# A graph-attention kernel with its front ordered anew, its transposes held two units ahead for longer, and its end summed in quarters

## The reference, cut to what matters

```
x = layernorm(x + L0(x, adj))        # masked softmax whose mask, with adj's ones on the diagonal, leaves only the own row
x = layernorm(x + L1(x, adj))

L1: h = x @ W.T + b_W
    e[i, j] = leaky_relu(h[i] @ a1 + h[j] @ a2 + b_a)      # slope 0.2
    p = softmax(where(adj > 0, e, -9e15), axis=1)          # 4096 x 4096
    return p @ h                                           # 4096 x 128
```

## Time and profile before

| | us |
|---|---|
| median of 3 runs | 253.71 (253.17 to 254.16) |
| the profiled execution | 255.0 |
| its span, first to last instruction | 253.2 |
| PE busy | 236.2 |
| DVE busy | 185.3 |
| ACT busy | 154.4 |
| POOL busy | 61.4 |

### The profile page before, as it was taken

How to read it: one execution, slowest core, us unless ns; L and a number is a source line. 1 busy time by engine, 2 the same in 40 slices (tenths; PEclk the granted TensorE clock), 3 DMA queues, 4 the chain that set the end, 5 groups by cost and what they waited for, 6 DMA issues and landing times.

```text
span 253.2 us, 4017 instructions
## 1 busy us (share of the span) xinstructions
PE 236.2 (93%) x1523; PEld 133.3 (53%) x1523; DVE 185.3 (73%) x284; ACT 154.4 (61%) x182; POOL 61.4 (24%) x104
## 2 busy tenths in 40 slices
PE   5959999499999999999999999999999999999980
PEld 4947675245555555555555555555555555555450
DVE  1378787967777777779768776977777778797433
ACT  2468978989067999170489994610899982220032
POOL 3284688999200000003030000002300000032122
PEclk9999999679999999999999999999999999999998
DMA  6999999999999999999589999998499920010102
GB/s 187 365 386 389 383 387 383 387 387 386 385 388 383 380 384 387 387 386 385 64 237 305 332 403 392 387 387 298 114 299 339 397 99 3 1 41 3 41 3 88
DMA packets 40939, 71.76 MB, mean 283 GB/s; under 512 B 5843, under 2 KB 6100, under 8 KB 40916
## 3 DMA queue, kind: packets, MB, share of 16 engines
q1 hardware_dynamic: 40480, 71.33, 79.2%
q10 hardware_dynamic: 436, 0.13, 0.2%
HBM read 69.36 MB, written 2.10 MB: 282 GB/s over the span
## 4 chain that ended last, share of the span: by engine, by line
PE 86%; POOL 3%; ACT 3%; DMA 2%; DVE 2%; issue 2%; ACTq 1%; POOLq 0%; DVEq 0%
PE banks L1202 67%; PE banks L1158 10%; PE banks L1217 3%; PE banks L1095 3%; DMA brow<-in_L_gnn_b_W_dram 2%; ACT a L737 2%; PE banks L1110 1%; POOL rstd L597 1%; PE banks L1081 1%; DVE y L1036 0%; POOL f_parts L636 0%; POOL xhat_st L602 0%; POOL frstd L646 0%; POOL feat L629 0%; DVE e_sb L938 0%
## 5 line engine op out<-in xcount | busy, mean ns | idle before, releaser
L1202 PE MATMUL banks<-e_sb,f_parts 128*128 128x512 f16 x768 | 186.1, 391 | 1.5 <-DVE e_sb L938 1.1
L926 DVE SCALAR_TENSOR_TENSOR e_sb<-R,cr_word,banks 128x1024 f32<-128x1024 f32 x124 | 153.8, 1275 | 30.9 <-PE banks L1158 28.3
L737 ACT ACTIVATE a<-a_sb,code_bias 128x2048 fp8e4<-128x2048 int32 x64 | 124.3, 1997 | 2.8 <-DMA a_sb<-in_adj_dram 2.1
L1202 PEld LDWEIGHTS banks<-e_sb,f_parts 128*128 128x128 f16 x768 | 71.6, 97 | 86.8 <-issue 4.0
L646 POOL TENSOR_TENSOR frstd<-frv,minus_half 128x4 f32<-128x4 f32 x8 | 8.1, 1012 | 168.9 <-DVE frv L962 167.6
L1158 PE MATMUL banks<-ident,a 128*128 128x128 f16 x496 | 38.0, 220 | 3.6 <-ACT a L737 3.6
L1158 PEld LDWEIGHTS banks<-ident,a 128*128 128x128 f16 x496 | 32.8, 98 | 15.4 <-ACT a L737 3.9
L728 ACT COPY R<-banks 128x512 f32<-128x512 f32 x8 | 4.7, 587 | 35.9 <-PE banks L1110 35.9
L753 ACT ACTIVATE junk<-y 128x128 f32<-128x128 f32 x28 | 8.3, 298 | 26.8 <-DVE y L953 26.8
L944 DVE RECIPROCAL rden<-banks 128x4 f32<-128x4 f32 x7 | 1.3, 183 | 12.2 <-PE banks L1217 12.2
L1095 PEld LDWEIGHTS banks<-m0c_um,x_tr 128*128 128x128 f32 x64 | 9.6, 224 | 0.8
(11 more groups left out here) (113 smaller groups left out, 101.9 us busy)
## 6 DMA issues: line engine op xcount, KB each, us to landing
a_sb<-in_adj_dram SPq DMA_DIRECT2D x64, 1024.0 KB, 12.4
x_sb<-in_x_dram SPq DMA_DIRECT2D x8, 256.0 KB, 9.9
out_dram<-out_sb SPq DMA_DIRECT2D x8, 256.0 KB, 5.8
w_nat<-in_L_gnn_W_dram ACTq DMA_DIRECT2D x1, 64.0 KB, 3.2
wv<-in_L_gnn_Wv_dram ACTq DMA_DIRECT2D x1, 64.0 KB, 3.1
acol<-in_L_gnn_a_vec_dram SPq DMA_DIRECT2D x1, 1.0 KB, 3.0
bcol<-in_L_gnn_b_W_dram ACTq DMA_DIRECT2D x1, 0.5 KB, 4.5
ba<-in_L_gnn_b_a_dram ACTq DMA_DIRECT2D x1, 0.0 KB
```

The costliest lines, as they stand in the source:

```text
L737: nc.scalar.activation(a8[:, n % 2, Q * h:Q * (h + 1), k * PW:(k + 1) * PW], a_parts[:, m % SLOTS, :, :], ACT.Relu, bias=code_bias[:, :], ...
L926: nc.vector.scalar_tensor_tensor(out=e_sb[:, k % NE, :], in0=R[:, g % 2, :], scalar=cr_word[:, 0, 2 * t + b:2 * t + b + 1], in1=ps_code[s ...
L1202: ins = nc.tensor.matmul(ps_acc[g % 2][h][:, :], f[:, j, :], e_half[:, k % NE, cols, part], start=(j == 0 and n == 0), stop=(j == T - 1 an ...
```

## The change

Three parts of the order change; no value that is computed does.

1. **Turning.** `FIRST` = 4 becomes `LATE` = 9. Up to slot 9, turn(s + 2) stands behind sums(s); in slot 9 turn(12) follows turn(11), and from slot 10 turn(s + 3) stands ahead of sums(s) as before.
2. **Front.** On SP load(0) goes ahead of load_x(1). On PE four keep-busy matmuls are gone, and x_turned(1) stands behind layer0(0), layer0(1) behind the two first half-turns, which now also wait for the copy of the second quad (it sits in the same bank). On ACT copy_xt(1) stands behind codes(0), and codes(1), copy_xt(2) ahead of exps(1). On DVE the first quad is divided and worded ahead of the second quad's statistics, and DVE instead of ACT copies the first half row of R. On POOL root(1) stands behind the first half of the features. The exponentials of the second quad go to another place in PSUM (bank 2).
3. **End.** Of the right 512 columns the last three units are summed in two quarters of 256. The first quarter goes to the old sums, the second (`LAST`) opens sums of its own in bank 7 (`ps_last`). ACT copies the whole right half after the first quarter; DVE adds `ps_last` to the copy. The output products stand ahead of each quarter's last unit, and the last two tiles' at the end.

```diff
-    FIRST = QUADS - 4
+    LATE = QUADS + 1
+    LAST = GW - 2 * P
...
 # sync
                 load_x(0)
                 sp.dma_start(acol[:, :], a_cols, ...)
+                load(0)
                 load_x(1)
-                load(0)
...
 # gpsimd
                 root(0)
+                features(0, 0)
                 root(1)
-                features(0, 0)
                 features(0, 1)
...
 # scalar
                 copy_xt(0)
-                copy_xt(1)
                 act.wait_ge(consts_ready, 12)
                 codes(0)
+                copy_xt(1)
                 exps(0)
+                codes(1)
+                copy_xt(2)
                 exps(1)
-                rows(0, 0, ps_row)
-                copy_xt(2)
-                codes(1)
                 rows(0, 1, ps_row2)
...
                 nc.scalar.copy(acc_t[:, 0:HW], ps_acc[g % 2][0][:, :]).then_inc(acc_copied, 1)
+                act.wait_ge(half_done, 2)
+                nc.scalar.copy(acc_t[:, HW:GW], ps_acc[g % 2][1][:, :]).then_inc(acc_copied, 1)
                 squares(g, 0)
-                act.wait_ge(half_done, 2)
-                for k in range(2):
-                    cols = slice(k * HW // 2, (k + 1) * HW // 2)
-                    nc.scalar.copy(acc_t[:, HW:GW][:, cols], ps_acc[g % 2][1][:, cols]).then_inc(acc_copied, 1)
...
 # vector
                 stats(0)
-                stats(1)
                 dve.wait_ge(rstd_ready, 1)
                 divide(0, scores)
                 divide(0, inner)
+                words(0)
+                stats(1)
+                dve.wait_ge(row_ready, 1)
+                nc.vector.tensor_copy(R[:, 0, 0:HW], ps_row[:, :]).then_inc(r_ready, 1)
+                half_edges(0, 0, 0)
+                half_edges(0, 1, 0)
                 dve.wait_ge(rstd_ready, 2)
                 divide(1, scores)
-                words(0)
+                half_edges(1, 0, 0)
                 words(1)
-                half_edges(0, 0, 0)
-                half_edges(0, 1, 0)
+                half_edges(1, 1, 0)
                 divide(1, inner)
-                half_edges(1, 0, 0)
-                half_edges(1, 1, 0)
...
+                    if k == 0:
+                        dve.wait_ge(half_done, 3)
+                        dve.wait_ge(acc_copied, 2 * G)
+                        nc.vector.tensor_tensor(acc_t[:, LAST:GW], ps_last[:, :], acc_t[:, LAST:GW],
+                                                ALU.add).then_inc(acc_copied, 1)
...
 # tensor
                 def half_turn(s, h):
 
                     pe.wait_ge(codes_ready, h + 1)
+                    pe.wait_ge(xt_copied, 2)
...
                 def last_sums():
...
-                    for s in units:
-                        for b in range(2):
-                            ins = products(s, b, 1)
-                        if s == S - HALVED:
-                            pe.wait_ge(acc_copied, 2 * G - 1)
-                            pe.wait_ge(y_ready, 2 * G - 2)
-                            projections(0, quad(0), range(Q)).then_inc(fin_mm, 1)
-                    ins.then_inc(half_done, 1)
                     for k in range(2):
-                        pe.wait_ge(acc_copied, 2 * G + k)
-                        projections(1, quad(4), range(2 * k, 2 * k + 2)).then_inc(fin_mm, 1)
+                        for s in units:
+                            if s == S - 1:
+                                if k == 0:
+                                    pe.wait_ge(acc_copied, 2 * G - 1)
+                                    pe.wait_ge(y_ready, 2 * G - 2)
+                                    projections(0, quad(0), range(Q)).then_inc(fin_mm, 1)
+                                else:
+                                    pe.wait_ge(acc_copied, 2 * G)
+                                    projections(1, quad(4), range(2)).then_inc(fin_mm, 1)
+                            for b in range(2):
+                                ins = products(s, b, (slice(HW, LAST), slice(LAST, GW))[k])
+                        ins.then_inc(half_done, 1)
+                    pe.wait_ge(acc_copied, 2 * G + 1)
+                    projections(1, quad(4), range(2, 4)).then_inc(fin_mm, 1)
...
                 x_turned(0)
                 weights(0)
+                weights(1)
+                layer0(0)
                 x_turned(1)
-                weights(1)
-                keep_busy(bank[0], 4)
-                layer0(0)
-                layer0(1)
                 half_turn(0, 0)
                 half_turn(1, 0)
+                layer0(1)
                 x_turned(2)
...
                 half_sums(0, 0)
-                spread(0, 1, ps_row2)
                 x_turned(3)
                 half_turn(0, 1)
+                spread(0, 1, ps_row2)
                 half_sums(1, 0)
...
-                    if FIRST < slot < S - NA:
+                    if LATE < slot < S - NA:
                         turn(slot + NA)
                     if slot < S - HALVED:
                         sums(slot)
...
-                    if slot <= FIRST:
+                    if slot <= LATE:
                         turn(slot + 2)
-                    if slot == FIRST:
+                    if slot == LATE:
                         turn(slot + 3)
```

More of the change, by code:

```diff
@@ L107, in graph_layers @@
         ps_row2 = bank[6]
-        ps_exp = [bank[4 + i][:, 256:256 + 2 * Q].rearrange("p (k q) -> p k q", k=2) for i in range(2)]
+        ps_exp = [bank[i][:, c:c + 2 * Q].rearrange("p (k q) -> p k q", k=2) for i, c in ((4, 256), (2, 160))]
+        ps_last = ps_row[:, 0:2 * P]
         ps_u = bank[5]
@@ L710, in exps @@
                         act.wait_ge(bias_ready, 4)
-                        act.wait_ge(at_half, i + 1)
+                        if i == 0:
+                            act.wait_ge(at_half, 1)
                         exp_c, exp_r = ps_exp[i][:, 0, :], ps_exp[i][:, 1, :]
@@ L1177, in half_sums @@
                         pe.wait_ge(p_half if h == 0 else p_ready, 2 * s + b + 1)
-                        ins = products(s, b, h)
+                        ins = products(s, b, halves[h])
                         if h == 1:
@@ L1193, in sums, with products @@
                         pe.wait_ge(p_ready, 2 * s + b + 1)
-                        products(s, b, 0)
-                        products(s, b, 1).then_inc(mm_done, 1)
-                def products(s, b, h):
+                        products(s, b, halves[0])
+                        products(s, b, halves[1]).then_inc(mm_done, 1)
+                def products(s, b, cols):
                     g, t = divmod(s, U)
                     k, j = 2 * s + b, 2 * t + b
-                    cols = slice(h * HW, (h + 1) * HW)
+                    h, first = divmod(cols.start, HW)
+                    dst, opened = ps_acc[g % 2][h][:, first:first + cols.stop - cols.start], j == 0
+                    if cols.start == LAST:
+                        dst, opened = ps_last[:, :], k == 2 * (S - HALVED)
                     for n, (f, part) in enumerate(((fl, 1), (fh, 1), (fh, 0))):
-                        ins = nc.tensor.matmul(ps_acc[g % 2][h][:, :], f[:, j, :], e_half[:, k % NE, cols, part],
-                                               start=(j == 0 and n == 0), stop=(j == T - 1 and n == 2))
+                        ins = nc.tensor.matmul(dst, f[:, j, :], e_half[:, k % NE, cols, part],
+                                               start=(opened and n == 0), stop=(j == T - 1 and n == 2))
                     return ins
@@ L1212, in project @@
                     projections(q, ps, range(Q)).then_inc(fin_mm, 1)
+                halves = slice(0, HW), slice(HW, GW)
                 def projections(q, ps, rs):
@@ L1226, in last_sums @@
                             pe.wait_ge(p_ready, 2 * s + b + 1)
-                            ins = products(s, b, 0)
+                            ins = products(s, b, slice(0, HW))
                     ins.then_inc(half_done, 1)
-                    for s in units:
-                        for b in range(2):
-                            ins = products(s, b, 1)
-                        if s == S - HALVED:
-                            pe.wait_ge(acc_copied, 2 * G - 1)
-                            pe.wait_ge(y_ready, 2 * G - 2)
-                            projections(0, quad(0), range(Q)).then_inc(fin_mm, 1)
-                    ins.then_inc(half_done, 1)
-                    for k in range(2):
-                        pe.wait_ge(acc_copied, 2 * G + k)
-                        projections(1, quad(4), range(2 * k, 2 * k + 2)).then_inc(fin_mm, 1)
+                    pe.wait_ge(r_ready, 2 * G)
+                    for k in range(2):
+                        for s in units:
[12 more added lines that the diff above has]
+                    projections(1, quad(4), range(2, 4)).then_inc(fin_mm, 1)
                 def keep_busy(ps, n):
```

## The result

| | before | after |
|---|---|---|
| median of 4 runs each, side by side | 253.6 us (253.17 to 254.16) | 250.88 us (250.39 to 251.41) |
| ratio | | 0.9892, 95% interval 0.9863 to 0.9920 |
| profiled execution, its own time | 255.0 us | 251.41 us |

The change makes the kernel about 1.1% faster, 2.7 us where 5.5 were forecast, and the time lies just above the range. Left out of every median and ratio are six executions of the experiments that count as slow: 255.36, 255.56 and 255.88 us of the kernel before, 256.12 of the end alone, and two of 351.61 and 839.51. A ratio with its interval is estimated over the executions; it is not the quotient of the two medians.

A forecast was written before the change was run, and what follows sets the result against it. PE, busy 93% of the span, was taken as the bound. Turning −6.4, front +0.5 and end −0.2 make −6.1: 248.9 from the profiled 255.0, 247.6 from the median; forecast 248.2, range 246.8 to 250.8 at 0.8.

The forecast's parts named there:

- the front's term: Start of the kernel, up to 26 us: the reordering makes it 0.5 us later, between −0.3 and +1.3.
- PE's new hole: Near 11.3 to 12.1 us, half_turn(0, 0) waits for the second quad's copy; claimed covered, since words(0) come at 14.8.
- Rival 2: Front: PE stops for 0.9 us, so its clock rises later; +0.5 to +0.9 more, 248.7 to 249.1; chance 0.12.
- what the turning is worth: Hole near 44 us: moving turn(8) behind sums(6) saves 6.4 us, of it 3.57 standing still and 2.7 half clock.
- Rival 5: Hole near 44 us: timed runs never lost clock, so only 3.6 of it counts, 250.4; chance 0.05.
- rival 1: The hole near 44 us comes back smaller as a POOL or DVE margin is overrun; 249.3 to 251.2; chance 0.13.
- front and end at their better bounds: Lower edge of the range, 246.8: front at −0.3 and the end gaining 0.5 us.
- every margin of slots 5 to 10: Middle: features, codes and edges are ready before PE's moved turns and sums need them, by 0.7 to 2.0 us.
- no wait for codes between 42 and 62: Sign of being right: PE waits for ACT's codes nowhere over 1 us between 42 and 62 us.
- full clock there: Sign of being right: the granted clock row is full between 42 and 62 us.
- the 256-column products: End: matmuls of 256 columns cost 113 ns each, 36 of them 4.07 us, the same as 18 long ones.
- the end's −0.2: End of the kernel: summing the last units in quarters gains 0.2 us, between −0.3 and +0.5.

## Why the prediction was wrong

**Failed: the front's term.** It was put at +0.5 and cost 1.73 in the profile and 1.4 between two kernels on one chip. The step that fails reads: PE's new hole "is covered, since words(0) come at 14.8, if layer0(1) and the rest then run at full clock". They did not run at full clock, and the words began at 13.61 and were done at 13.99, so there was less idle time to hide in than assumed. Rival 2 had this mechanism, at 0.12 and with 1.2 us of cover subtracted. By it the front costs 1.0 to 1.4, the size that was measured. The forecast also had two inputs wrong, which the rival shares. x(1) kept PE waiting for 0.39 us, for a load put ahead of it that brought codes(0) forward only from 9.79 to 9.61; and layer0(0) came earlier than assumed (7.84 for 8.76), which opened the stop further: x_turned(1) no longer stands ahead of it either, and that was not taken off. Filling the stops took the 1.7 away again, so the clock behind the stops is shown as the cause, not argued. The Trainium skill, "TensorE: Matmul & The Clock Gate", section "What's actually happening", says that the throttled state is the default and activity releases it; this trace agrees (layer0(1) 2.05 us behind the stops, 1.31 with them filled).

**Mis-sized: what the turning is worth against the median.** Against the profiled execution it was −6.2 to −6.4 of span for −6.4. But 2.7 of that is half clock, which the kernel before loses in some executions and not in others. The sum from the profiled execution's own time (255.0 − 6.4 = 248.6) met the turning alone (248.54); the sum from the median, 247.3, did not. The forecast of 248.2 went half way to the median and should have stayed at 248.9. Rival 5 had the mechanism, as all or nothing. That its 250.4 lies close to the measured time is luck: it gives the turning 3.6 us, and alone the turning took off 5.4 (253.92 − 248.54) on one chip and 6.1 (254.93 − 248.83) on another; the front took 1.4 back. The range of rival 1 holds the measured time too, but no margin was overrun. Two slips of the working change nothing: front and end at their better bounds give 246.7, not 246.8, and rival 1 begins at 249.2, not 249.3.

**Right:** every margin of slots 5 to 10, no wait for codes between 42 and 62, full clock there, the 256-column products (114 ns for 113). The estimate of 98 ns from the figures of the Trainium skill, "TensorE: Matmul & The Clock Gate", section "Back-to-back issue gap", does not fit. **Small miss:** the end's −0.2 went into the 0.2 us between the last product's end and DVE's start.

Put together: 248.9, and 0.9 to 1.2 more for the front and 0.2 for the end, make 250.0 to 250.3. The changed kernel measured 250.46 and 250.88; the last 0.2 to 0.9 are not assigned. A longer last store with the new end could hold some of it, which no run shows.

## What to carry to other kernels

Where two engines' orders change at the start of a kernel, cost TensorE's half clock first: two stops of under 1 us ahead of its work on the chain cost more than all the reordering saved, and a few products that nobody reads gave it back. Take a term that was read from one execution off that execution's time, and ask whether the others pay it at all. And measure the parts apart: here one part of three gave everything, one gave nothing, and one took 1.4 us back.

## What the runs showed of the hardware

A stop of TensorE of the same length (3.57 us, to the digit) was followed by half clock in two profiles (the kernel before and the end alone, 1.03 us for turn(8) in both) and by full clock in one (the front alone, 0.62). Over the executions of the kernel before, the time goes with the mean granted clock: 251.38 to 252.13 us at 0.993 to 0.994, 253.1 to 255.0 at 0.983 to 0.989, 254.2 to 255.3 at 0.976 to 0.982. And the granted clock is shown as full in the front, where durations are those of the lower level: both windows of the changed kernel below have 1.00 in the column behind the engines, while the eight products of layer0(1) at 13.04 take 2.05 us and the eight half turns at 12.23 take 1.01, with 0.61 in the kernel before.

```profile
8.00:13.00 5.00, 3.82 (x20) 3.15 (x21) 2.03 (x11) 2.54 (x3) 2.52 (x6) 1.00 1.04 396
13.00:18.00 5.00, 5.00 (x33) 4.88 (x31) 2.30 (x11) 3.17 (x5) 3.24 (x6) 1.00 1.05 387
```
